# Cross-attention scores of a transformer block: one fp32 product against three products of rounded and remaining parts

## The chip, the cores and the metric

The kernel runs on one core of a Trainium2 chip. A core has five engines, each with its own instruction stream: TensorE (PE in the profile; matmuls and transposes, results into PSUM), VectorE (DVE), ScalarE (ACT), GpSimd (POOL), and SyncE (SP), which here only issues DMAs. They share an on-chip memory (SBUF) and wait for each other through semaphores. Within an engine, instructions run in the order in which the program lists them. PSUM has eight banks of 512 fp32 columns on 128 partitions.

The metric is the device time of one execution. Before the change: 1,482.18 us, the median of three runs (1,481.14 to 1,485.02).

## The reference

Eight batches of 512 tokens with 256 features, and a context of 64 rows a batch. In the cut, what matters is the first half:

```python
def _L0_xattn_ref(inputs_q, inputs_kv, Wq, bq, Wk, bk, Wv, bv, Wo, bo):   # H, HD = 16, 64
    q = jnp.einsum('bqm,mhd->bqhd', inputs_q, Wq) + bq
    k = jnp.einsum('bkm,mhd->bkhd', inputs_kv, Wk) + bk
    v = jnp.einsum('bkm,mhd->bkhd', inputs_kv, Wv) + bv
    q = q / jnp.sqrt(jnp.asarray(HD, q.dtype))
    attn = jax.nn.softmax(jnp.einsum('bqhd,bkhd->bhqk', q, k), axis=-1)
    out = jnp.einsum('bhqk,bkhd->bqhd', attn, v)
    return jnp.einsum('bqhd,hdm->bqm', out, Wo) + bo
...
x = x + _L0_xattn_ref(_layernorm(x), ctx_1024, ...)
x = x + _L0_ffn_ref(_layernorm(x), ...)   # dense path (causal attention, 16 heads of 16; SiLU FFN of 1024) + sparse path (8 experts, top 2)
```

## The kernel before

The batches are taken one after the other in eight *walks*, numbered 0 to 7, of about 143 us each; after the last comes a stretch with the experts and the final sum. Walk b handles the cross attention, the queries and keys, the routing and the maxima of batch b, and beside that the causal attention and the feed-forward network of batch b - 1. Walk 0 has no batch before it. The order of the steps is a list written by hand (`CROSS`, `SCORES`, `STEPS`), and every engine goes through the same list and does its own share of each step. So an instruction that waits holds up all that comes behind it on its engine.

The head of a walk is about the cross attention. Its scores are x times a folded matrix: for each pair of heads, the transposed query weights `wqT` times the block-diagonal keys `k_bd` of this batch. The steps are:

- `m` 0 to 3 (L871): the fold, each of four products into bank 0, 1, 2 or 3; the results go to `m_sb` in SBUF, 2 x 1024 columns. ScalarE copies `m` 0 and 2 (L1170), VectorE `m` 1 and 3 (L1432).
- `x_turn` 0 and 1 (L844): TensorE transposes the normalised x into banks 0 and 1, after the copies have freed them; ScalarE copies to `xnT` (L1146).
- `shift` 1 (L979): small transposes for the batch before (the row maxima of its second half of heads), in bank 5; VectorE copies them (L1555), SyncE sends them on.
- `bqk` (L880): bias products; `sc` (L996), `va` (L1009), `out_t` (L1020): scores, values and outputs of the causal attention of the batch before, put between the steps of the cross attention.
- `cs` t, half (L901): the cross scores of token tile t (four tiles of 128) and one half of the heads, two fp32 products of 128 rows of `xnT` by 512 columns of `m_sb` into one bank. The profile shows each fp32 product as two records. Both halves then go through VectorE (L1441 add, L1443 maximum, L1444 subtract), ScalarE (L1184 exponential), VectorE (L1451 sum, L1452 reciprocal) and GpSimd (L721 normalise); `ct` (L913) and `cv` (L920) are the transposes and the value products.

GpSimd also makes the causal cuts (L703) that `va` waits for, an addition of a bias to x (L716), and sums for the output. The feed-forward network's up projection (L1051) already multiplies in three products of a rounded part and a remaining part, in the type `float32r`; each product is one record of 512 columns. VectorE makes the remaining part of its input by a subtraction of the rounded part from the PSUM bank (L1570). At the end of a walk VectorE scales the feed-forward result (L1624).

Of the kernel before, what the change touches and what calls it, by code (L numbers as in the profile page):

```python
# [17 lines left out]
P = 128  # L18
# [33 lines left out]
    x_in=16, kv_in=64, stats=4, stats1=1, mv1=1, rstd1=1, xn1=1, xT1=2, xnT=2, bq=1,  # L52
    m_ps=4, m_act=2, m_dve=2, bqk_ps=2, bqk_sb=2, vw_ps=4, vw_sb=4,
# [4 lines left out]
    gmax=1, gexp=1, mask=1, rank_ps=1, slot=1, xk=1, scat=128, dve_step=42, pool_a=4, pool_n=1,  # L58
    a_ps=32, a_max=32, m_part=2, mT_ps=2, mT_sb=2, m_row0=48, m_row1=48,
    b_ps=G * UNITS, b_exp=G * UNITS, b_cut=G * UNITS, va_ps=G * CHUNKS, av_sb=4, avT_ps=4, o_rec=4, o_nrm=4,  # L60
    oT_ps=2, oT_sb=2, wo_ps=2, wo_sq=2, wo_ri=1, wo_n=2, hb=1, h=2, yb=1, hT_ps=2, hT_sb=2, hT_lo=2,
    fu_ps=16, fu_th=8, fu_u=8, fu_g=8, fd_ps=8, fd_sq=1, fd_ri=1, fd_n=1, y=1, y_out=16, pool_f=2,
# [144 lines left out]
def xattn_ffn(nc, A, out):  # L207
    per = PER
    counted = {}
    with ExitStack() as ctx:  # L210
# [10 lines left out]
        p0 = {n: sem("p0_" + n) for n in ("w_first", "bias_ps", "w_early", "w_mid", "w_late", "w_turned", "w_up", "kv0_ps", "norms", "split_hi", "split", "ident", "const", "iota", "tr_ps", "tr_sb", "kv_ps", "kv_sb", "bk")}  # L221

        moe = {n: sem("moe_" + n) for n in ("table_step", "table", "ids_off", "ids", "ew_in", "zero", "gate", "xT_ps", "xT", "up_ps", "th", "u", "g", "gT_ps", "gT", "dn_ps", "eo")}
# [43 lines left out]
        with nc.sbuf_tensor("hT", [P, 2, KD, S], F32R) as hT:  # L267
            pass
        room = sb("room", [P, 28672])
# [9 lines left out]
        m_sb = part(0, 2048).rearrange("p (k n) -> p k n", k=KD)  # L279
# [41 lines left out]
        w_heads = yb[:, :, :].rearrange("p t d -> p (t d)").rearrange("p (i k n) -> p i k n", i=2, k=KD)  # L321
        xnT = sb("xnT", [P, KD, S])
        xn2T = sb("xn2T", [P, KD, S])
# [68 lines left out]
        vt_d = internal("vt_d", (PAIRS, P, B * CK))  # L392
        parts_d = internal("parts_d", (3, 2, HD, H // KD, KD, S), BF16)
# [13 lines left out]
        def before(eng, b, name):  # L407

            if not (isinstance(b, int) and b == 0):
                eng.wait_ge(sems[name], b * per[name] + AHEAD.get(name, 0))  # L410

# [36 lines left out]
        def _(sp):  # L448
# [74 lines left out]
            def batch(b, c, end=False, only=None):  # L523
# [5 lines left out]
                if b is not None:  # L529
                    if c is None:  # L530
                        load_late_weights()
                    elif b != B - 1:
                        load_kv(b + 1)
# [13 lines left out]
                    send_shifts(b, 0)  # L547
                    if c is None:
# [59 lines left out]
        def _(pool):  # L608
# [44 lines left out]

            def batch(b, c, end=False, only=None):
# [1026 lines left out]
```

## Time and profile before

| | |
|---|---|
| median of the three runs | 1,482.18 us (1,481.14 to 1,485.02) |
| span of the profiled execution | 1,484.5 us, first to last instruction |
| runs' own times, in order | 1,485.02, 1,482.18, 1,481.14 us |
| TensorE busy, matmuls | 1,362.4 us, 92% |
| mean granted TensorE clock | 0.976 |

No separate time was taken around the profiled execution beside its span; the span is used for it. "Busy" is the time in which at least one instruction of the engine is shown running. Matmuls are pipelined, so two records in a row overlap by their tails: the start of one to the start of the next is what a product takes in a stream. A row of the view in order of time has the start, the length, the engine, the line, the operation, the names and shapes, and the count of instructions merged in it; in brackets stands the idle time ahead of it and what ended it.

### The profile page before, as it was taken

What the parts mean: (1) busy time and instruction counts of PE and PEld (TensorE: products, weight loads), DVE (VectorE), ACT (ScalarE), POOL (GpSimd) and SP (SyncE); (2) the same over time, 40 slices, a digit from 0 to 9 for tenths busy, and PEclk for the clock granted to TensorE, in tenths of its full rate; (3) what the DMA queues carried; (4) which work ended last, traced back from release to release, by engine and by line L of the source; (5) the groups of instructions that cost most, each with busy time, mean ns of one, the idle gap of its engine ahead of it and who ended that gap; (6) DMA issues with size and microseconds to landing.
All of it is one profiled execution on the core that took longest, in us unless ns stands there. A gap on an engine that the chain in (4) does not pass through costs nothing. (4 is left out here: it accounts for less than half of the span.)

```text
span 1484.5 us, 22385 instructions
## 1 busy us (share of the span) xinstructions
PE 1362.4 (92%) x7229; PEld 882.2 (59%) x7230; DVE 810.0 (55%) x1654; ACT 575.1 (39%) x1214; POOL 600.2 (40%) x1051
## 2 busy tenths in 40 slices
PE   6887899899999989998999899999999889999995
PEld 5543556666665666566656665666566346666674
DVE  2625554764585368536753675467537623333348
ACT  2231553055306521642265126503640443344446
POOL 4312353254325342634254225423542445555544
PEclk9998899999999999999999999999999899999997
DMA  6053204110501050106000500140022533322245
GB/s 213 1 153 132 86 1 121 52 30 1 142 30 30 1 156 16 30 8 160 20 15 30 141 17 15 51 121 17 1 83 74 162 107 128 129 87 85 85 186 193
DMA packets 78297, 115.39 MB, mean 78 GB/s; under 512 B 24840, under 2 KB 66208, under 8 KB 75648
## 3 DMA queue, kind: packets, MB, share of 16 engines
q1 hardware_dynamic: 67888, 79.69, 17.9%
q10 hardware_dynamic: 3840, 16.78, 4.2%
q0 software_dynamic: 6480, 17.77, 3.3%
q8 instruction: 52, 0.85, 0.2%
q14 instruction: 37, 0.30, 0.1%
HBM read 70.22 MB, written 43.59 MB: 77 GB/s over the span
## 5 line engine op out<-in xcount | busy, mean ns | idle before, releaser
L1540 DVE TENSOR_REDUCE nm<-ps 128x2 f32<-128x256 f32 (+3 forms) x256 | 202.5, 819 | 85.6 <-PE ps L970 79.5
L1229 ACT ACTIVATE room<-ps 128x512 f32<-128x512 f32 x320 | 179.8, 599 | 151.3 <-PE ps L996 151.1
L1051 PE MATMUL ps<-hT,w 128*128 128x512 f32 x768 | 206.5, 412 | 0.0
L703 POOL TENSOR_SCALAR_AFFINE_SELECT room<-room 128x256 f32<-128x256 f32 (+1 forms) x320 | 121.0, 390 | 136.4 <-ACT room L1229 131.7
L969 PE MATMUL ps<-room 96*128 96x128 bf16 (+3 forms) x512 | 127.9, 312 | 35.7 <-DMA room<-parts_d 17.8
L1051 PEld LDWEIGHTS ps<-hT,w 128*128 128x128 f32 x768 | 140.4, 190 | 32.1 <-DVE hT L1570 2.0
L1061 PE MATMUL ps<-w,room 128*128 128x256 f32 x512 | 137.8, 400 | 7.8 <-DVE room L1591 7.8
L1253 ACT ACTIVATE room<-ps 128x512 f32<-128x512 f32 x64 | 37.2, 593 | 277.2 <-PE ps L1051 277.2
L1087 PE MATMUL ps<-room 128*128 x284 | 135.4, 599 | 1.8 <-ACT room L1281 1.8
L920 PE MATMUL ps<-room 128*128 128x256 f32 x512 | 123.1, 384 | 2.8 <-ACT room L1190 1.8
L901 PE MATMUL ps<-room,xnT 128*128 128x512 f32 x256 | 122.0, 601 | 0.0
L996 PE MATMUL ps<-room 99*128 99x384 bf16 (+3 forms) x512 | 111.0, 306 | 8.7 <-ACT room L1229 6.4
L969 PEld LDWEIGHTS ps<-room 96*128 96x128 bf16 x512 | 50.9, 100 | 97.9 <-DVE nm L1540 41.1
L920 PEld LDWEIGHTS ps<-room 128*128 128x128 f32 x512 | 93.8, 190 | 22.7 <-issue 6.7
L1061 PEld LDWEIGHTS ps<-w,room 128*128 128x128 f32 x512 | 91.9, 195 | 24.1 <-DVE room L1591 11.5
L970 PE MATMUL ps<-mask_qk,ident_b 128*128 128x128 bf16 x512 | 104.6, 225 | 0.0
L1634 DVE COPY room<-ps 128x256 f32<-128x256 f32 x71 | 30.1, 424 | 125.9 <-PE ps L1095 117.7
L1441 DVE TENSOR_TENSOR room<-ps,room 128x1024 f32<-128x1024 f32 x32 | 39.1, 1222 | 106.0 <-PE ps L901 106.0
L996 PEld LDWEIGHTS ps<-room 99*128 99x128 bf16 x512 | 42.9, 98 | 88.0 <-issue 44.7
L1009 PE MATMUL ps<-room,v_aug 128*32 128x512 f32 (+3 forms) x1024 | 90.6, 449 | 3.0 <-POOL room L703 2.0
L652 POOL TENSOR_TENSOR spare_p<-neg_half 128x1 f32<-128x1 f32 x95 | 18.3, 192 | 179.7 <-DVE room L1533 114.6
L794 POOL DMA_INDIRECT pair_d<-room,ids_u x71 | 71.8, 1011 | 33.7 <-issue 30.5
(236 smaller groups left out, 2360.1 us busy)
## 6 DMA issues: line engine op xcount, KB each, us to landing
room<-parts_d SPq DMA_DIRECT2D x48, 256.0 KB, 8.7
room<-parts_d ACTq DMA_DIRECT2D x48, 256.0 KB, 6.2
room<-xs_d SPq DMA_DIRECT2D x71, 129.0 KB
parts_d<-room SPq DMA_DIRECT2D x64, 128.0 KB, 1.8
room<-pair_d SPq DMA_DIRECT2D x8, 1024.0 KB, 7.8
room<-in_L_ffn_ew SPq DMA_DIRECT2D x24, 256.0 KB, 5.5
xin<-in_x SPq DMA_DIRECT2D x8, 512.0 KB, 11.3
parts_d<-xnT SPq DMA_DIRECT2D x32, 128.0 KB, 1.8
```

The lines of the kernel that those rows point to most:

```text
L703: done(g.affine_select(out=w, in_=w, compare_op=ALU.is_ge, fill=0.0, base=0, pattern=[[0, 2]] * (blocks - 1) + [[1, P]], channel_multiplie ...
L901: last = mm(bank(half), xnT[:, k, t * P:(t + 1) * P], m_sb[:, k, half * 512:(half + 1) * 512], start=(k == 0), stop=(k == KD - 1))
L920: last = mm(bank(3, D), pT[:, t % 2, a * P:(a + 1) * P], vw[:, a, :], start=(a == 0), stop=(a == PAIRS - 1))
L969: mm(bank(o, n), q_rep[0:KREP, rep_at(h), t * P:n], k_rep[0:KREP, rep_at(h), 0:n], start=True, stop=False)
L970: last = mm(bank(o, P, t * P), ident_b[:, :], mask_qk[:, :], start=False, stop=True)
L996: last = mm(ps[:, o:o + S - kb * P], k_rep[0:KREP + MROWS, h, kb * P:(kb + 1) * P], q_rep[0:KREP + MROWS, h, kb * P:S], start=True, stop=T ...
L1009: last = mm(ps[32 * j:32 * j + 32, 4 * 512 + kb * P:5 * 512], v_aug[:, v_at(kb, 4 * grp + j):v_at(kb, 4 * grp + j) + 32], prob[:, at:at + ...
L1051: last = mm(bank(up_banks(b, m)[i]), w[:, x, k, m * P:(m + 1) * P], hT[:, y, k, :], start=((x, y, k) == terms[0]), stop=((x, y, k) == term ...
L1061: last = mm(bank((6, 7)[half], D, t % 2 * D), gT[:, m % 2, t * P:(t + 1) * P], w2[:, m, :], start=(m == 0 and t % 2 == 0), stop=(m == FB - ...
L1087: last = mm(bank(2 + i % 2), xsT[:, i % 2, k * P:(k + 1) * P], ew[:, bass.ds(at + k * 2 * D, 2 * D)], start=(k == 0), stop=(k == KD - 1))
L1229: done(fn(prob[:, u * 512:(u + 1) * 512], bank(score_bank(b) + n % 2), ACT.Exp), "b_exp")
L1540: done(v.tensor_reduce(nm[:, t, 2 * hp:2 * hp + 2], pair_ps, AX.X, ALU.max, negate=True), "a_max")
```

## The change

The cross scores are computed from a rounded part (`_hi`, type `float32r`) and a remaining part (`_lo`) of both x and the folded weights, by three products for each of the two depth blocks: hi x hi, lo x hi, hi x lo. For that, ScalarE now copies all four folds and both turns of x, rounding, and VectorE subtracts each copy from its bank. The turns of x use banks 4 and 5 and no longer wait for copies of the fold. The shift's transposes, in bank 5 too, wait for the remaining part of x. The remaining part of the folded weights is written over `wqT`, so `wqT` is kept in DRAM by a store in walk 0 and loaded again once a walk (walks 1 to 6); in walk 0 another place is used. Counters of VectorE's and GpSimd's inner steps, which had one semaphore for each purpose, now share one for each engine.

```diff
+        m_lo_first = over_room("m_lo_first", 22528, [P, PAIRS, D])
+        m_lo = over_room("m_lo", 7168, [P, PAIRS, D])
...
@@ SyncE
+                        sp.wait_ge(p0["tr_sb"], 6)
+                        sp.dma_start(wqT_d, wqT.rearrange("p a n -> p (a n)")).then_inc(p0["wq_kept"], 16)
...
                     send_shifts(b, 0)
+                    if c is not None and b != B - 1:
+                        need(sp, b, "sc_ps", T)
+                        sp.dma_start(wqT.rearrange("p a n -> p (a n)"), wqT_d).then_inc(p0["wq_in"], 16)
@@ TensorE
-                        turn(b, xh, (0, 1), lambda t2: [("xn1", 1), (("m_act", "m_dve")[t2], 1)], "xT1", step[1:])
+                        turn(b, xh, (4, 5), lambda t2: [("xn1", 1)], "xT1", step[1:])
...
+                            if b >= 2:
+                                pe.wait_ge(p0["wq_in"], 16 * (b - 1))
...
-                        need(pe, b, ("m_act", "m_dve")[i], 2)
+                        need(pe, b, "m_lo", 3 + i)
...
-                            need(pe, b, "m_act", 2)
-                            need(pe, b, "m_dve", 2)
-                            need(pe, b, "xnT", 2)
+                            need(pe, b, "m_lo", 4)
+                            need(pe, b, "xnT_lo", 2)
...
-                        for k in range(KD):
-                            last = mm(bank(half), xnT[:, k, t * P:(t + 1) * P], m_sb[:, k, half * 512:(half + 1) * 512], start=(k == 0), stop=(k == KD - 1))
+                        for x, y, k in [(x, y, k) for x, y in ((0, 0), (1, 0), (0, 1)) for k in range(KD)]:
+                            rows = m_low(b)[:, half * 4:half * 4 + 4, k * P:(k + 1) * P] if y else m_hi[:, k, half * 512:(half + 1) * 512].rearrange("p (a n) -> p a n", a=4)
+                            last = mm(bank(half).rearrange("p (a n) -> p a n", a=4), (xnT_hi, xnT_lo)[x][:, k, t * P:(t + 1) * P], rows,
+                                      start=((x, y, k) == (0, 0, 0)), stop=((x, y, k) == (0, 1, KD - 1)))
...
@@ TensorE, the shift's transposes
                             need(pe, b, "a_max", 19)
+                        elif b is not None:
+                            need(pe, b, "xnT_lo", 2)
@@ ScalarE
-                        spread(b, xnT, (0, 1), "xT1", "xnT", step[1:])
-                    elif kind == "m" and step[1] % 2 == 0:
+                        spread(b, xnT_hi, (4, 5), "xT1", "xnT", step[1:])
+                    elif kind == "m":
                         i = step[1]
                         need(act, b, "m_ps", i + 1)
-                        done(fn(m_sb[:, i // 2, 0:512], bank(i), ACT.Copy), "m_act")
+                        done(fn(m_hi[:, i // 2, i % 2 * 512:(i % 2 + 1) * 512], bank(i), ACT.Copy), "m_hi")
@@ VectorE
-                    elif kind == "m" and step[1] % 2:
+                    elif kind == "m":
                         i = step[1]
-                        need(dve, b, "m_ps", i + 1)
-                        done(v.tensor_copy(m_sb[:, i // 2, 512:1024], bank(i)), "m_dve")
+                        need(dve, b, "m_hi", i + 1)
+                        if b and i == 0:
+                            dve.wait_ge(p0["wq_kept"], 16)
+                        done(v.tensor_tensor(m_low(b)[:, i % 2 * 4:i % 2 * 4 + 4, i // 2 * P:(i // 2 + 1) * P], bank(i).rearrange("p (a n) -> p a n", a=4),
+                                             m_hi[:, i // 2, i % 2 * 512:(i % 2 + 1) * 512].bitcast(F32).rearrange("p (a n) -> p a n", a=4), ALU.subtract), "m_lo")
+                    elif kind == "x_turn":
+                        t2 = step[1]
+                        need(dve, b, "xnT", t2 + 1)
+                        cols = slice(t2 * 2 * P, (t2 + 1) * 2 * P)
+                        done(v.tensor_tensor(xnT_lo[:, :, cols], bank(4 + t2).rearrange("p (k n) -> p k n", k=KD),
+                                             xnT_hi[:, :, cols].bitcast(F32), ALU.subtract), "xnT_lo")
```

The order of TensorE at the head of a walk, before. Line numbers are those of the kernel before; a count stands behind the row, and in brackets what it waits for.

```order
L871 MATMUL ps<-room 128x128 [waits a_max]
L871 MATMUL ps<-room 128x128 x7
L844 MATMUL ps<-ident,room 128x128 [waits m_dve,xn1]
L844 MATMUL ps<-ident,room 128x128 x3
L979 MATMUL ps<-ident_b,nparts 128x128 [waits m_part]
L979 MATMUL ps<-ident_b,nparts 128x128 x3
L880 MATMUL ps<-room 128x128 [waits m_act,bq]
```

The same place after. L900 is the fold, L871 the turn of x, L1011 the shift's transposes, L909 the bias product (in the line numbers of the changed kernel).

```order
L900 MATMUL ps<-room 128x128 [waits a_max]
L900 MATMUL ps<-room 128x128 x7
L871 MATMUL ps<-ident,room 128x128 [waits xn1]
L871 MATMUL ps<-ident,room 128x128 x3
L1011 MATMUL ps<-ident_b,nparts 128x128 [waits xnT_lo,m_part]
L1011 MATMUL ps<-ident_b,nparts 128x128 x3
L909 MATMUL ps<-room 128x128 [waits m_lo,bq]
```

Nothing has moved on TensorE there; the waits are others. The turn has one less, the shift's transposes and the bias product wait for VectorE's subtractions.

VectorE at the same place, before: the scaling of the feed-forward result, two copies of the fold, the copy of the shift.

```order
L1551 TENSOR_TENSOR nparts<-nr,nparts 128x4x8 [waits dve_step]
L1624 SCALAR_TENSOR_TENSOR room<-ps,ri,fw_bc 128x256 [waits fd_ri]
L1624 SCALAR_TENSOR_TENSOR room<-ps,ri,fw_bc 128x256 x3
L1432 COPY room<-ps 128x512 [waits m_ps] x2
L1555 COPY mT<-ps 48x512 [waits mT_ps]
L1441 TENSOR_TENSOR room<-ps,room 128x1024 [waits bqk_sb,sc_ps]
```

And after, with the subtractions at L1456 (fold) and L1462 (x):

```order
L1653 SCALAR_TENSOR_TENSOR room<-ps,ri,fw_bc 128x256 [waits fd_ri]
L1653 SCALAR_TENSOR_TENSOR room<-ps,ri,fw_bc 128x256 x3
L1456 TENSOR_TENSOR m_lo<-ps,m_hi 128x4x128 [waits p0_wq_kept,m_hi]
L1456 TENSOR_TENSOR m_lo<-ps,m_hi 128x4x128 [waits m_hi]
L1462 TENSOR_TENSOR xnT_lo<-ps,xnT_hi 128x2x256 [waits xnT]
L1456 TENSOR_TENSOR m_lo<-ps,m_hi 128x4x128 [waits m_hi] x2
L1462 TENSOR_TENSOR xnT_lo<-ps,xnT_hi 128x2x256 [waits xnT]
L1585 COPY mT<-ps 48x512 [waits mT_ps]
L1472 TENSOR_TENSOR room<-ps,room 128x1024 [waits bqk_sb,sc_ps]
```

Six subtractions stand where two copies stood, between the scaling and the copy of the shift.

SyncE's queue late in a walk, after. L470 loads the next x, L484 sends the shift's rows, L570 is the added load, L593 stores the output of the batch before.

```order
L564 DMA room<-parts_d 16x8192 x5
L470 DMA xin<-in_x 128x4x256 [waits xn1,xb]
L484 DMA room<-mT 1x8x512 [waits mT_sb]
L484 DMA room<-mT 1x8x512 x2
L570 DMA room<-wqT_d 128x2048 [waits sc_ps]
L593 DMA y_d<-hb 128x1024 [waits y]
```

The load is between the sends of the first half of the shift and the store of the output.

## Rows read from the trace of the kernel before

**Rows 1.** Busy time and share of the span, by engine, with instruction counts.

```profile
PE 1362.4 (92%) x7229; PEld 882.2 (59%) x7230; DVE 810.0 (55%) x1654; ACT 575.1 (39%) x1214; POOL 600.2 (40%) x1051
```

**Rows 2.** TensorE's waits: who for whom, us in total, times, longest.

```profile
PE ps L1009 <- POOL room L703: 2.0, 7, 0.3
```

**Rows 3.** Instructions grouped by line: count, busy us, mean ns.

```profile
L901 PE MATMUL ps<-room,xnT 128*128 128x512 f32 x256 | 122.0, 601 | 0.0
```

**Rows 4.** TensorE in order of time, walk 3: cross scores and their successors.

```profile
456.34 1.94 PE L901 MATMUL ps<-room,xnT 128*128 128x512 f32 x4
458.11 0.60 PE L996 MATMUL ps<-room 99*128 99x384 bf16 x4
...
466.08 1.99 PE L901 MATMUL ps<-room,xnT 128*128 128x512 f32 x4
467.90 0.60 PE L996 MATMUL ps<-room 99*128 99x512 bf16 x2
```

**Rows 5.** TensorE in order of time, walk 3: up projection in three products.

```profile
531.03 5.87 PE L1051 MATMUL ps<-hT,w 128*128 128x512 f32 x24
...
568.51 1.64 PE L1051 MATMUL ps<-hT,w 128*128 128x512 f32 x6
569.99 0.23 PE L969 MATMUL ps<-room 96*128 96x128 bf16 x1
```

**Rows 6.** All engines in order of time, walk 3, behind the second tile's scores.

```profile
467.70 1.90 POOL L721 TENSOR_TENSOR room<-room,crec 128x1024 f32<-128x1024 f32 x1 [0.29 <-DVE crec L1452]
...
471.88 3.10 POOL L703 TENSOR_SCALAR_AFFINE_SELECT room<-room 128x128 f32<-128x128 f32 x6
...
472.49 1.06 PE L1009 MATMUL ps<-room,v_aug 128*32 128x512 f32 x8 [0.29 <-POOL room L703]
```

**Rows 7.** All engines in order of time, head of walk 3.

```profile
448.58 1.65 DVE L1624 SCALAR_TENSOR_TENSOR room<-ps,ri,fw_bc 128x256 f32<-128x256 f32 x4
...
450.16 0.68 DVE L1432 COPY room<-ps 128x512 f32<-128x512 f32 x1
...
451.16 0.69 DVE L1432 COPY room<-ps 128x512 f32<-128x512 f32 x1 [0.33 <-PE ps L871]
451.45 0.39 PE L979 MATMUL ps<-ident_b,nparts 128*128 128x128 bf16 x4
451.65 0.60 ACT L1146 ACTIVATE xnT<-ps 128x512 f32<-128x512 f32 x1 [0.78 <-PE ps L844]
```

**Rows 8.** VectorE in order of time, walk 3: subtraction of a rounded part.

```profile
529.69 1.29 DVE L1570 TENSOR_TENSOR hT<-ps,hT 128x512 fp32r<-128x512 f32 x2 [2.16 <-ACT hT L1146]
```

**Rows 9.** VectorE and TensorE in order of time, head of walk 1.

```profile
164.82 1.28 DVE L1432 COPY room<-ps 128x512 f32<-128x512 f32 x2
165.65 0.63 PE L844 MATMUL ps<-ident,room 128*128 128x128 f32 x4 [0.56 <-DVE room L1432]
166.12 0.39 PE L979 MATMUL ps<-ident_b,nparts 128*128 128x128 bf16 x4
```

**Rows 10.** SyncE's sends, the next fold, and loads of 1,024 KB (median us to landing).

```profile
576.05 2.06 SPq L466 DMA_DIRECT2D room<-mT  x3
...
589.61 2.02 PE L871 MATMUL ps<-room 128*128 128x128 f32 x16 [0.44 <-DVE nm L1540]
...
room<-in_L_ffn_w SPq DMA_DIRECT2D x2, 1024.0 KB, 6.9
...
room<-in_L_xattn_Wo SPq DMA_DIRECT2D x1, 1024.0 KB, 11.2
```

**Rows 11.** VectorE and TensorE in order of time, walk 0.

```profile
32.66 0.69 DVE L1432 COPY room<-ps 128x512 f32<-128x512 f32 x1 [3.19 <-PE ps L871]
...
34.69 3.60 PE L901 MATMUL ps<-room,xnT 128*128 128x512 f32 x8
...
56.70 0.65 PE L913 MATMUL ps<-ident,room 128*128 128x128 f32 x4 [1.29 <-DVE x L1457]
```

**Rows 12.** Two stretches: busy us by engine, granted clock, DMA share, GB/s.

```profile
156.00:158.00 2.00, 1.75 (x7) 0.90 (x8) 1.47 (x3) 0.00 (x0) 0.00 (x0) 0.50 0.58 238
545.50:548.70 3.20, 0.01 (x1) 0.00 (x0) 0.50 (x3) 0.60 (x1) 0.19 (x1) 1.00 0.70 168
```

More of the change, by code:

```diff
@@ L1371, in make_table @@
-                chain(v.tensor_reduce(expert, begun[:, :, :], AX.X, ALU.add))
-                chain(v.tensor_tensor(begun[:, :, :], begun[:, :, :], starts, ALU.mult))
-                chain(v.tensor_reduce(start, begun[:, :, :], AX.X, ALU.max))
-                chain(v.tensor_scalar(expert, expert, -1.0, None, ALU.add))
-                chain(v.tensor_tensor(row, tile_c, start, ALU.subtract))
-                chain(v.tensor_scalar(row, row, float(P), None, ALU.mult))
-                chain(v.scalar_tensor_tensor(row, expert, float(REG), row, ALU.mult, ALU.add))
@@ L1378, in make_table @@
-                chain(v.tensor_scalar(table[:, 0, :], expert, float(EW), None, ALU.mult))
-                chain(v.tensor_scalar(start, tile_no[:, :], total, None, ALU.is_lt))
-                chain(v.tensor_scalar(row, row, -float(E * REG), None, ALU.add))
-                chain(v.tensor_tensor(row, row, start, ALU.mult))
+                link(v.tensor_tensor(begun[:, :, :], tile_c.unsqueeze(2).to_broadcast(by_expert), starts, ALU.is_ge))
+                link(v.tensor_reduce(expert, begun[:, :, :], AX.X, ALU.add))
@@ new lines, in make_table @@
+                link(v.tensor_tensor(begun[:, :, :], begun[:, :, :], starts, ALU.mult))
+                link(v.tensor_reduce(start, begun[:, :, :], AX.X, ALU.max))
+                link(v.tensor_scalar(expert, expert, -1.0, None, ALU.add))
+                link(v.tensor_tensor(row, tile_c, start, ALU.subtract))
+                link(v.tensor_scalar(row, row, float(P), None, ALU.mult))
+                link(v.scalar_tensor_tensor(row, expert, float(REG), row, ALU.mult, ALU.add))
+                link(v.tensor_scalar(table[:, 0, :], expert, float(EW), None, ALU.mult))
@@ L1383, in make_table @@
+                link(v.tensor_scalar(start, tile_no[:, :], total, None, ALU.is_lt))
+                link(v.tensor_scalar(row, row, -float(E * REG), None, ALU.add))
+                link(v.tensor_tensor(row, row, start, ALU.mult))
                 v.tensor_scalar(table[:, 1, :], row, float(E * REG), None, ALU.add).then_inc(moe["table"], 1)
[L1384 to L1385 removed]
+                link(v.tensor_scalar(start, tile_no[:, :], total, None, ALU.is_ge))
@@ L1416, in batch @@
                             last = v.bn_stats(st1[:, t, :], xin[:, t, :])
-                        done(last, "stats1")
-                        need(dve, n, "stats1", 1)
+                        link(last)
                         carry_wait()
```

90 lines of the change are left out of this document (46 added, 44 removed).

## The prediction

> **What bounds the kernel now.** I read the shares of busy time first. TensorE is busy for 92% of the span, VectorE for 55%, ScalarE and GpSimd for about 40% [rows 1]. The chain of waits does not help here: it only follows the last few microseconds, in the mixing stage at the end. So I took the list of waits of TensorE and asked what it ever waits for. No item of it is large; a small one is to matter below, seven waits for GpSimd of 0.3 us at most [rows 2]. For the rest the walks are TensorE working through its own order. A microsecond of matmul that goes is worth a microsecond, unless the next thing in the order then waits; and a wait put in TensorE's order costs what it lasts.
>
> **The products.** A walk has eight score banks (four token tiles, two halves). Before, a bank is two fp32 products, shown as four records of 512 columns: 256 records in all, 122.0 us [rows 3]. The up projection already uses the three-product scheme, with one record a product. Busy time counts overlapping tails, so I price by start to next start. Two banks of the score line take 1.77 us (456.34 to 458.11) and 1.82 us (466.08 to 467.90) [rows 4]; the six others of that walk lie between 1.72 and 1.87, and 1.77 is the middle. A group of six products of the up projection takes 1.48 us (568.51 to 569.99) [rows 5]. The new bank is six such products with the same shapes and the same kind of operands, so I take 1.48, and a gain of 0.29 us a bank, 2.3 us a walk. Bounds: the run of 24 such products in 5.87 us with a last record of 0.39 gives a pitch of 0.238 us, hence 1.43 a bank and a gain of 0.34; the shortest old bank of 1.72 gives 0.24. The rows of the remainder of the folded weights are now read in four pieces of 128 columns with a step between them. No row shows such a read; I cost it at nothing and keep 0 to 0.05 us a bank in the range, since all else in the product is as in the up projection.
>
> The Trainium skill speaks of the rate too ("TensorE: Matmul & The Clock Gate", section "Wait — 56ns, not 53.3ns?"): back-to-back matmuls start every 215.7 ns at 512 columns. By that a bank would be 1.29 us, an estimate, and the gain 0.48 us. The rows give 0.238 to 0.25 for this very form, so they decide. The rival on cheap products below is what it would be otherwise.
>
> **Where a gain is not kept.** In walks 1 to 7 the attention of the batch before is interleaved. After the second tile's scores TensorE comes to a value product at 472.49 that already waits 0.29 us for GpSimd [rows 6]. GpSimd gets there by a chain of its own: the normalisation from 467.70 (1.90 us), the bias addition (2.38 us), then the causal cuts from 471.88 that the product needs. It starts from a reciprocal that hangs on the first tile and not on the second, whose matmuls run beside it. Two banks made shorter by 0.29 us make TensorE arrive 0.58 us sooner and wait 0.58 us longer. The seven waits of at most 0.3 us [rows 2] are this place in each of the seven walks. So six banks of eight pay: 6 x 0.29 = 1.74 us a walk. The other places have no such wait before; I looked at the cuts and exponentials behind each pair of banks and they end 0.1 us or more before they are needed.
>
> **What is added.** At the head of a walk, TensorE folds the weights (four groups), and turns x (two groups). Before, ScalarE and VectorE share the copies: ScalarE has four, VectorE two. After, ScalarE makes a rounded copy of all six and VectorE subtracts each of the six from its bank. TensorE then has, in its order, the small transposes of the shift. They now use a bank that the second turn of x occupies, so they wait for the sixth subtraction, and everything behind them waits with them: the bias products, the first scores of the previous batch, the cross scores.
>
> When does the sixth end? Take walk 3 [rows 7]. VectorE is late here: the scaling of the feed-forward output starts at 448.58 and holds it until the first copy at 450.16. Nothing of this is changed. The subtractions then follow back to back. Each has one input in PSUM, one in SBUF and 512 elements; the pair of the same form in the feed-forward stage takes 1.29 us for two [rows 8], so a pitch of 0.60 and 0.69 for the last. ScalarE is not later: the fourth fold is done when the second copy of VectorE is let go, at 451.16; ScalarE needs 0.6 us for it and 0.6 us more for the turn (the length of its copy at 451.65), 452.4, while VectorE gets to the sixth only at 453.16. So 450.16 + 5 x 0.60 + 0.69 = 453.85. In walk 1 a copy of VectorE that starts at 164.82 and ends about 165.5 lets a transpose of TensorE go at 165.65 [rows 9], so 0.15 us for the release: 454.0. Before, the transposes start at 451.45. The wait is 2.55 us. No work of TensorE fills it, as its order is fixed. Bounds: 2.3 (the queue of subtractions starts no earlier, but the release is free) to 3.1 us (a pitch of 0.69 instead of 0.60).
>
> Walk 1 is different and gives the same. VectorE there splits weights until 164.82, the two copies start then, and the transposes run at 166.12 [rows 9]. After: 164.82 + 3.69 + 0.15 = 168.66, 2.54 us later.
>
> Who else waits? What the shift writes is needed only by the third group of heads, well into the walk. The exponentials and cuts are let go by TensorE and move with it. GpSimd, which is behind at the head of a walk, has time to catch up, but its first cuts are not waited for in either case.
>
> **The reload.** The subtractions overwrite the transposed weights, so six times a 1,024 KB load is added on SyncE's queue, behind the three small sends that SyncE issues from 576.05 for 2.06 us. Its condition, the last scores, is long met. It is issued at about 578.1. TensorE folds at 589.61 [rows 10]: 11.5 us. The nearest 1,024 KB loads landed in 6.9 us, and in 11.2 us where a whole set of weights was loading at once; here the DMA is quiet. I take 7 us, which is hidden with 4 us to spare; at 11.2 us it would just be at the edge. What follows it in SyncE's queue is the store of the output, at the next walk's head. The first store of these weights, and the two new semaphores, wait for nothing that isn't long done. The other edits (shared counters in place of one for each step) change names, not the number of waits.
>
> **The first walk** has no attention beside it. The fourth fold is copied at 32.66 [rows 11]; now a rounded copy (0.60) and a subtraction (0.69) stand in a row there, to 33.95, and the second bias group starts after it at about 34.1 and takes about 1 us, so the scores start near 35.1 instead of 34.69: 0.4 us later. Two banks in a row are 3.60 us there and will be 0.39 + 11 x 0.238 = 3.01. Tile 0 gives 0.6 - 0.4, tile 1 gives 0.6, tile 3 gives 0.6, and tile 2 nothing, since TensorE waits 1.29 us behind it for VectorE [rows 11]. Together 1.4 us.
>
> **Sum.** Seven walks at 2.55 - 1.74 = 0.81 are 5.7 us; less 1.4 us, so 4.3 us slower. The profiled execution has a span of 1,484.5 us, 2.3 us above the median of 1,482.18 and just under the highest run. From 1,484.5 the sum leads to 1,488.8; the same 4.3 us on the median give 1,486.5, and that is the forecast. It is 0.29%, so it lies on the edge: I count over 0.3% (4.4 us) as what a measurement of this kernel can tell from no change.
>
> **Rivals.**
> *Cheap products (faster).* If a product of the new form starts every 0.215 us, half of the pitch of an old record ((3.60 - 0.59) / 7 = 0.43 [rows 11]), a bank is 1.29 and gains 0.48. Seven walks at 2.55 - 2.88 = -0.33 are -2.3, the first walk -2.2, together -4.5: 1,477.7. For it: nothing but that the columns allow it. Against: the run of 24 [rows 5]. It decides below 0.22 us.
> *Every bank pays.* If the wait for GpSimd moves with TensorE, 0.58 x 7 = 4.1 us come back: 1,482.4, no change. Against: GpSimd is busy without a gap from 467.70 to 472.49.
> *A longer wait.* At 3.1 us in place of 2.55 the seven walks lose 3.9 us more: 1,490.4. For it: six dependences across three engines, each a possible 0.1 us.
> *The reload is late.* From 11.5 us on, each microsecond costs six: 14 us would make 1,501. Against: the quiet DMA.
> *The clock falls.* A granted clock of 0.50, the lower level of 1.2 GHz, stands at 156 to 158 us [rows 12], in the first walk's end, where TensorE had waited again and again. If the new idle did this in each walk and it lasted 3 us, it would cost 1.5 us, 7 x 1.5 = 10.5: 1,497. Against: TensorE is idle for 3.2 us in walk 3 (545.5 to 548.7), after steady work, and the clock is 1.00 in that stretch [rows 12]. The Trainium skill (the same page, section "HAM oscillation — how this bites in real kernels") says that idle gaps throttle the engine again; by that rule a longer gap than this might do it, and the trace shows that one of 3.2 us did not.
>
> **How the numbers follow.** Forecast 0.50 (0.30 of it within 0.3%, 0.20 beyond); every bank pays 0.13 (no change); cheap products 0.15 (faster); longer wait 0.13, late reload 0.05, clock 0.04 (slower). So faster 0.15, same 0.43, slower 0.42. The forecast's own range, with 0.24 to 0.34 a bank and 2.3 to 3.1 us of wait, is 1,482 to 1,493; to hold eight of ten it has to reach into the faster rival and over the longer wait: 1,479 to 1,493.
>
> **What would show it.** Per walk: the score products busy for about 13 us instead of 15.4; TensorE idle for 2.5 us before the shift's transposes, released by VectorE's sixth subtraction; the wait for GpSimd before the value product grown from 0.3 to 0.9 us; no wait for the reloaded weights before the fold. I am wrong if the transposes start less than 2 us after the second turn, if a bank takes under 1.4 or over 1.6 us, or if the fold waits for a DMA.

## The result, and the profile after

| | before | after |
|---|---|---|
| median, us | 1,482.31 (20 runs) | 1,488.95 (20 runs) |
| lowest to highest, us | 1,474.4 to 1,489.83 | 1,480.97 to 1,503.78 |
| span of the profiled execution, us | 1,484.5 | 1,486.7 (its own time 1,488.45) |
| ratio after to before, with its 95% interval | | 1.0042 [1.0025, 1.0059] |

The changed kernel is slower by 0.42%, about 6.2 us, with 3.7 to 8.7 us as the interval. The forecast was 4.3 us and 1,486.5, its range 1,479 to 1,493: the time lies in it. Slower had a chance of 0.42, no change (within 0.3%) one of 0.43, faster 0.15. The prediction saw the two mechanisms and came near their sizes; it missed a third, which the experiments below bring out. The run of 1,503.78 us, over 1.5% above the fastest, is not in the ratio.

Busy time by engine, the row that answers to [rows 1]:

```profile
PE 1345.9 (91%) x7357; PEld 904.4 (61%) x7358; DVE 828.7 (56%) x1686; ACT 583.2 (39%) x1230; POOL 601.7 (40%) x1051
```

TensorE is busy for 16.5 us less than before [rows 1], and yet the span is 2.2 us longer. So TensorE's idle time grew by 18.7 us. The waits of TensorE (who for whom, us in total, times, longest) say where:

```profile
PE ps L1011 <- DVE xnT_lo L1462: 18.5, 7, 3.6
...
PE ps L999 <- DMA room<-parts_d: 15.1, 7, 3.3
...
PE ps L1041 <- POOL room L730: 6.2, 7, 0.9
```

The first is new: 18.5 us before the shift's transposes. The third was 2.0 us [rows 2]. The second stands in both kernels (14 to 18 us in the traces of either) and varies from one execution to the next; where I compare walks below, I take it out.

The score products, grouped by line and names, answer to [rows 3]:

```profile
L930 PE MATMUL ps<-m_hi,xnT_hi 128*128 128x512 f32 x128 | 46.7, 446 | 0.0
L930 PE MATMUL ps<-m_hi,xnT_lo 128*128 128x512 f32 x128 | 40.2, 395 | 0.0
L930 PE MATMUL ps<-m_lo,xnT_hi 128*128 128x512 f32 x112 | 35.2, 395 | 0.0
L930 PE MATMUL ps<-m_lo_first,xnT_hi 128*128 128x512 f32 x16 | 5.0, 395 | 0.0
```

There are 384 records where there were 256. The busy times of the four groups add up to 127.1 us, more than the 122.0 before, but records of two groups overlap and are counted in both. All records of the line taken together are busy for less (us, TensorE, weight load, granted clock, DMA share, GB/s):

```profile
0.00:1487.00 1487.00, 105.75 (x384) 68.86 (x384) 0.97 0.27 83
```

That is 13.2 us a walk where it was 15.2, and 16.2 us less in all, nearly all that TensorE's busy time lost. TensorE in order of time at the head of walk 3 (start, length, count, and in brackets the idle time before it):

```profile
447.35 2.02 PE L900 MATMUL ps<-room 128*128 128x128 f32 x16 [0.44 <-DVE nm L1570]
...
454.52 0.38 PE L1011 MATMUL ps<-ident_b,nparts 128*128 128x128 bf16 x4 [2.48 <-DVE xnT_lo L1462]
...
457.12 0.76 PE L930 MATMUL ps<-m_hi,xnT_hi 128*128 128x512 f32 x2
...
459.08 0.71 PE L930 MATMUL ps<-m_hi,xnT_hi 128*128 128x512 f32 x2
459.63 0.63 PE L930 MATMUL ps<-m_hi,xnT_lo 128*128 128x512 f32 x2
460.09 0.63 PE L930 MATMUL ps<-m_lo,xnT_hi 128*128 128x512 f32 x2
460.56 0.61 PE L1028 MATMUL ps<-room 99*128 99x384 bf16 x4
```

This bank runs from 459.08 to 460.56, 1.48 us, against 1.77 in [rows 4]. From start to next start the eight banks of the walk take 1.48 to 1.60 us, where they took 1.72 to 1.87. The transposes wait 2.48 us. What VectorE does meanwhile, against [rows 7]:

```profile
449.14 1.65 DVE L1653 SCALAR_TENSOR_TENSOR room<-ps,ri,fw_bc 128x256 f32<-128x256 f32 x4
450.71 1.28 DVE L1456 TENSOR_TENSOR m_lo<-ps,m_hi 128x512 fp32r<-128x512 f32 x2
451.90 0.68 DVE L1462 TENSOR_TENSOR xnT_lo<-ps,xnT_hi 128x512 fp32r<-128x512 f32 x1
452.50 1.27 DVE L1456 TENSOR_TENSOR m_lo<-ps,m_hi 128x512 fp32r<-128x512 f32 x2
453.69 0.68 DVE L1462 TENSOR_TENSOR xnT_lo<-ps,xnT_hi 128x512 fp32r<-128x512 f32 x1
```

Six subtractions without a gap, 3.66 us from the first start to the last end; 0.15 us after it the transposes start. And behind the second tile, all engines in order of time, against [rows 6]:

```profile
470.17 1.91 POOL L748 TENSOR_TENSOR room<-room,crec 128x1024 f32<-128x1024 f32 x1 [0.28 <-DVE crec L1483]
...
474.35 3.10 POOL L730 TENSOR_SCALAR_AFFINE_SELECT room<-room 128x128 f32<-128x128 f32 x6
...
474.95 1.07 PE L1041 MATMUL ps<-room,v_aug 128*32 128x512 f32 x8 [0.89 <-POOL room L730]
```

TensorE waits 0.89 us there where it waited 0.29. From the normalisation to the value product it is 4.78 us, as before (467.70 to 472.49): GpSimd's chain is as long as it was, and TensorE comes to its end sooner. The reload, among the DMA issues (KB each, median us to landing):

```profile
room<-wqT_d SPq DMA_DIRECT2D x6, 1024.0 KB, 4.9
```

In walk 3 it is issued at 580.11 for the fold at 591.55; the median of the six lands 4.9 us after its issue. No wait of TensorE for it is listed.

### The profile page after: what moved, and what is told of

Same layout as the page of the kernel before. It is cut to its first block and busy times, and to the rows that moved or that the text cites. A ratio compares the mean times of both kernels' runs of the same rounds, so it can differ in the third digit from the quotient of the medians.

```text
span 1486.7 us, 22694 instructions
## 1 busy us (share of the span) xinstructions
PE 1345.9 (91%) x7357; PEld 904.4 (61%) x7358; DVE 828.7 (56%) x1686; ACT 583.2 (39%) x1230; POOL 601.7 (40%) x1051
## 5 line engine op out<-in xcount | busy, mean ns | idle before, releaser
L1083 PEld LDWEIGHTS ps<-hT,w 128*128 128x128 f32 x768 | 141.8, 192 | 32.4 <-DVE hT L1599 2.0
L950 PEld LDWEIGHTS ps<-room 128*128 128x128 f32 x512 | 93.8, 190 | 22.0 <-issue 5.8
L1663 DVE COPY room<-ps 128x256 f32<-128x256 f32 x71 | 30.1, 424 | 125.8 <-PE ps L1127 125.8
L1028 PEld LDWEIGHTS ps<-room 99*128 99x128 bf16 x512 | 39.7, 99 | 75.3 <-issue 38.2
L1119 PEld LDWEIGHTS ps<-room 128*128 128x128 f32 x284 | 50.3, 189 | 45.8 <-issue 41.2
```

The costliest lines, as they stand in the source:

```text
L950: last = mm(bank(3, D), pT[:, t % 2, a * P:(a + 1) * P], vw[:, a, :], start=(a == 0), stop=(a == PAIRS - 1))
L1028: last = mm(ps[:, o:o + S - kb * P], k_rep[0:KREP + MROWS, h, kb * P:(kb + 1) * P], q_rep[0:KREP + MROWS, h, kb * P:S], start=True, stop=T ...
L1083: last = mm(bank(up_banks(b, m)[i]), w[:, x, k, m * P:(m + 1) * P], hT[:, y, k, :], start=((x, y, k) == terms[0]), stop=((x, y, k) == term ...
L1119: last = mm(bank(2 + i % 2), xsT[:, i % 2, k * P:(k + 1) * P], ew[:, bass.ds(at + k * 2 * D, 2 * D)], start=(k == 0), stop=(k == KD - 1))
```

## The experiments

For walks I give the length from one fold's start to the next, of the shortest walk in which the granted clock stays at 1.00, less TensorE's wait for the DMA in it; I call that the clean walk. It is 139.6 us before (142.81 less 3.2, walk 3) and 140.3 after (141.98 less 1.7, walk 4): the new walk is 0.7 us longer. Not every walk at full clock is as short: a wait of TensorE for VectorE in the feed-forward stage is 0.5 us in these two, and 1.6 in walk 4 before and 1.5 in walk 2 after. It varies in both kernels.

### Is it the wait for the sixth subtraction?

**e1_swap.** The two turned halves of x change banks, so that the transposes' bank hangs on the first half and the third subtraction.

```diff
-  turn(b, xh, (4, 5), ...)            # TensorE
+  turn(b, xh, (5, 4), ...)
-  need(pe, b, "xnT_lo", 2)            # before the shift's transposes
+  need(pe, b, "xnT_lo", 1)
-  spread(b, xnT_hi, (4, 5), ...)      # ScalarE
+  spread(b, xnT_hi, (5, 4), ...)
-  v.tensor_tensor(xnT_lo[...], bank(4 + t2)...)
+  v.tensor_tensor(xnT_lo[...], bank(5 - t2)...)
```

> The changed kernel with the two turns of x in banks 5 and 4 instead of 4 and 5, so that the shift's transposes (bank 5) wait for the third of the six subtractions and not for the sixth. If VectorE's queue of subtractions sets the head of the walk: the wait before the shift falls from 2.5 to about 0.8 us, new waits of about 0.4 us each come before the bias products or the first score bank, and the scores start 1.2 to 1.4 us earlier in walks 1 to 7: 8 to 10 us less than the changed kernel, so about 2 to 4 us below the kernel before. If the reload or the shared counters cost the time: the same time as the changed kernel.

Measured: 1,476.44 us (12 runs), ratio to the kernel before 0.996 [0.9938, 0.9981]; so 12.5 us less than the changed kernel by the medians. TensorE, head of walk 3:

```profile
443.64 2.02 PE L900 MATMUL ps<-room 128*128 128x128 f32 x16 [0.44 <-DVE nm L1570]
...
449.02 0.38 PE L1011 MATMUL ps<-ident_b,nparts 128*128 128x128 bf16 x4 [0.70 <-DVE xnT_lo L1462]
449.62 1.13 PE L909 MATMUL ps<-room 128*128 128x128 f32 x8 [0.21 <-DVE m_lo L1456]
...
452.02 0.76 PE L930 MATMUL ps<-m_hi,xnT_hi 128*128 128x512 f32 x2
```

The wait is 0.70 and not 2.48 us, and from fold to scores it takes 8.38 us (9.77 after, 7.38 before). The clean walk is 138.8 us, 1.4 less. Six such walks are 8.5 us. Walk 1 gives more, 3.3 us (145.70 for 149.00): its wait goes from 3.57 to 1.53 us, and with it goes a fall of the clock (below).

### What are the products alone worth?

**e2_products.** The kernel before, with six rounded products a bank in place of the fp32 ones. The products of the remaining parts, and the making of those parts, are left out (the rounded product is run three times).

```diff
-  for k in range(KD):
-      last = mm(bank(half), xnT[...], m_sb[...], ...)
+  for r, k in [(r, k) for r in range(3) for k in range(KD)]:
+      last = mm(bank(half), xnT_hi[...], m_hi[...], ...)
```

> The kernel before, but each score bank made by six products of the rounded part of x and of the rounded folded weights (the remaining parts are left out, the same rounded operands taken three times). No subtraction, no reload, banks and waits as before. If the products gain 0.29 us a bank and two banks of eight are lost to the wait for GpSimd: 7 x 1.74 + about 2 to 3 in the first walk, 14 to 15 us less than before, with the wait for GpSimd at 0.9 us. If all eight banks pay: 18 to 19 us less. If the products gain nothing: no change.

Measured: 1,463.43 us (6 runs), ratio 0.9884 [0.985, 0.9918], 17 us less by the ratio and 18 by the medians. The time alone is nearer to my "all eight banks pay" (18 to 19) than to "two are lost" (14 to 15). The trace decides. The wait for GpSimd in the list of TensorE's waits:

```profile
PE ps L1013 <- POOL room L706: 6.3, 7, 0.9
```

The wait for GpSimd grows to 0.9 us with the products alone, so it is they that uncover it. The clean walk is 137.7 us, 1.9 less than before; I had 1.74. Laid beside the kernel before, what follows a bank in walk 3 comes 0.30 to 0.33 us sooner for each of the eight banks, 2.5 us in all, and 0.60 goes at the wait for GpSimd: 1.9. So a bank gives a little more than my 0.29, and two banks of eight are lost, as forecast. Seven walks are 13 us, and walk 0 is 4.8 us shorter (130.31 for 135.12). Of that, 1.4 us lie ahead of its scores and 2.4 in a wait for ScalarE at its end (2.38 for 4.74 us), which is 3.05 us in e7_bias_only with the old products; so some of it belongs to that one execution of before and not to the products. The price of the subtractions, 140.3 less 137.7, is 2.6 us a walk.

### Does the reload cost anything?

**e3_reload.** The kernel before, with the store of the transposed weights, the six reloads, the fold's wait for them, and the shared counters.

```diff
+  sp.dma_start(wqT_d, wqT.rearrange("p a n -> p (a n)"))...
...
+  if c is not None and b != B - 1:
+      need(sp, b, "sc_ps", T)
+      sp.dma_start(wqT.rearrange("p a n -> p (a n)"), wqT_d)...
...
+  if b >= 2:
+      pe.wait_ge(p0["wq_in"], 16 * (b - 1))
```

> The kernel before with the store of the transposed weights, the reload once a walk and the shared counters, and nothing else of the change. If the reload is hidden: no wait for it before the fold, and the time of the kernel before within 0.3%. If the reload or the counters are what makes the changed kernel slower: about 6 us more than before.

Measured: 1,481.69 us (12 runs), ratio 0.9995 [0.9975, 1.0015]. The reload landed in 4.9 us here too, and no wait of TensorE for it is listed. It costs nothing that this can tell, which is from 3.7 us less to 2.2 more.

### Is it the length of the wait?

**e6_two_more.** The changed kernel, with each of the two subtractions of x made twice: two more instructions in VectorE's queue, one of them ahead of the fourth, both ahead of the transposes.

```diff
+  link(v.tensor_tensor(xnT_lo[:, :, cols], bank(4 + t2)..., xnT_hi[:, :, cols]..., ALU.subtract))
   done(v.tensor_tensor(xnT_lo[:, :, cols], bank(4 + t2)..., xnT_hi[:, :, cols]..., ALU.subtract), "xnT_lo")
```

> The changed kernel with each of the two subtractions of x made twice by VectorE, so two more in the queue of six. If that queue sets the head of the walk: the wait before the shift grows from 2.5 by 1.2 to 1.5 us in walks 2 to 7, 8 to 10 us more than the changed kernel, about 1,498 us. If a wait of that length also lets TensorE's clock fall to the lower level, as it did behind the wait of 3.6 us in walk 1 of the changed kernel (0.50 from 166 to 170 us), each walk in which that happens takes about 2 us more: up to 1,510 us, and the granted clock behind the shift shows 0.5. If ScalarE or a release sets the head: the time of the changed kernel.

Measured: 1,509.21 us (5 runs), ratio 1.0168 [1.0137, 1.0198]. In TensorE's waits:

```profile
PE ps L1011 <- DVE xnT_lo L1464: 29.7, 7, 6.0
```

That is 11.2 us more than after in seven waits (six of 3.94 or 3.95 us, 1.46 more each), but the time is 20 us more by the medians (19 by the ratios). The shortest walk less its wait for the DMA is 143.3 us (145.0 less 1.7), 3.0 longer, twice what the wait adds. So something is paid beside the wait. The next section has it.

### The clock behind the wait

**a1_again, a2_again, a3_again.** The changed kernel once more in three executions, unedited, to see whether the clock falls behind the transposes.

> The changed kernel once more, unchanged, for another profile. If the waits of 2.5 us before the shift let the clock fall in some executions and not in others, a granted clock of 0.5 stands behind the shift's transposes in one or more of walks 2 to 7 in some of the three. If only longer waits (3.6 us in walk 1, over 3 us for the DMA) do it, none of walks 2 to 7 shows it there, and the falls stand behind the DMA waits as in the kernel before.

> A second further profile of the unchanged changed kernel, with the same expectations as a1_again: a fall of the clock behind a 2.5 us wait of walks 2 to 7, or falls behind longer waits alone.

> A third further profile of the unchanged changed kernel, with the same expectations as a1_again: a fall of the clock behind a 2.5 us wait of walks 2 to 7, or falls behind longer waits alone.

Measured: 1,493.01, 1,494.96 and 1,491.85 us, with spans of 1,491.2, 1,493.2 and 1,490.1; the kernel before ran in 1,483.17 beside them (one run each, and not on the chip of the other experiments). First the four microseconds behind the transposes' start in the profiled execution of after, walks 1 and 3 (length; busy us of TensorE, weight load, VectorE, ScalarE, GpSimd; granted clock; DMA share; GB/s):

```profile
165.78:169.78 4.00, 4.00 (x24) 3.51 (x24) 0.42 (x1) 1.36 (x3) 0.29 (x1) 0.62 0.03 6
...
454.52:458.52 4.00, 4.00 (x29) 3.40 (x29) 0.42 (x1) 2.61 (x5) 1.72 (x3) 1.00 0.23 90
```

The five other walks show 1.00 as well. The same stretch of all seven walks in a2_again:

```profile
168.04:172.04 4.00, 4.00 (x20) 3.85 (x21) 0.42 (x1) 1.08 (x2) 0.29 (x1) 0.50 0.03 6
315.19:319.19 4.00, 4.00 (x29) 3.40 (x29) 0.42 (x1) 2.61 (x5) 1.72 (x3) 1.00 0.23 90
457.74:461.74 4.00, 4.00 (x22) 3.73 (x23) 0.42 (x1) 1.09 (x3) 1.41 (x2) 0.60 0.23 90
601.60:605.60 4.00, 4.00 (x29) 3.41 (x29) 0.42 (x1) 2.60 (x5) 1.73 (x3) 1.00 0.25 95
743.46:747.46 4.00, 4.00 (x22) 3.56 (x23) 0.42 (x1) 1.22 (x3) 1.43 (x2) 0.60 0.23 90
891.44:895.44 4.00, 4.00 (x24) 3.72 (x24) 0.42 (x1) 1.19 (x3) 1.43 (x2) 0.62 0.23 90
1038.22:1042.22 4.00, 4.00 (x24) 3.71 (x24) 0.42 (x1) 1.19 (x3) 1.43 (x2) 0.63 0.23 90
```

TensorE is busy without a gap in both, but in four of walks 2 to 7 it does 22 to 24 matmuls where it does 29 at full clock. TensorE in order of time there, walk 3 of a2_again:

```profile
457.74 0.59 PE L1011 MATMUL ps<-ident_b,nparts 128*128 128x128 bf16 x4 [2.49 <-DVE xnT_lo L1462]
458.12 2.02 PE L909 MATMUL ps<-room 128*128 128x128 f32 x8
...
461.78 0.81 PE L930 MATMUL ps<-m_hi,xnT_hi 128*128 128x512 f32 x2
```

From the transposes to the scores it is 4.04 us, against 2.60 in the profiled execution (454.52 to 457.12, the start of its first record of scores), after a wait of the same length to 0.01 us. In the eleven falls of walks 2 to 7 in the three traces, fold to scores takes 1.0 to 1.6 us more; in six of them it is 1.40 to 1.55, and a fall that comes late runs on behind the first scores. I counted the falls at this place in all four executions:

| execution | walk 1 | falls in walks 2 to 7 | span, us |
|---|---|---|---|
| after | 0.62 | 0 | 1,486.7 |
| a3_again | 0.57 | 4 (0.61, 0.57, 0.66, 0.63 in walks 3, 5, 6, 7) | 1,490.1 |
| a1_again | 0.62 | 3 (0.59, 0.57, 0.64 in walks 3, 5, 6) | 1,491.2 |
| a2_again | 0.50 | 4 (0.60, 0.60, 0.62, 0.63 in walks 3, 5, 6, 7) | 1,493.2 |
| e1_swap (waits of 1.5 and 0.7 us) | 1.00 | 0 | 1,470.8 |
| e6_two_more (waits of 6.0 and 3.9 us) | 0.50 | 6 (0.50 to 0.59) | 1,503.5 |

In e6_two_more all walks fall: 1.46 + 1.5 = 3.0 us a walk, the 3.0 found above. In e1_swap none does, not even in walk 1: there 3.3 us go, which with the 8.5 us of the six others makes 11.8, against 12.5 between the medians and 12.2 by the ratios.

The falls at this place can't simply be added to the span, because the clock falls behind the waits for the DMA too, with the old products as with the new. In walk 3 of after it does:

```profile
549.10:552.40 3.30, 3.21 (x11) 2.34 (x12) 1.02 (x2) 0.00 (x0) 1.08 (x1) 0.50 0.10 33
```

The three other executions have their fall of walk 3 behind the transposes and none later in that walk, and all four walks are equally long, 141.7 to 141.8 us less the wait for the DMA, 1.5 above the clean walk. So in this walk one fall took the place of the other. All falls have to be counted. Here is the time at the lower level (0.50) from the transposes of walk 1 to the fold of walk 7:

| execution | at the lower level, us | falls behind the transposes in walks 2 to 6 | length of walks 2 to 6, us |
|---|---|---|---|
| before | 13.7 | | 716.4 |
| e3_reload | 17.1 | | 716.9 |
| e7_bias_only (below) | 13.7 | | 713.2 |
| after | 20.5 | 0 | 719.5 |
| a3_again | 17.1 | 3 | 718.2 |
| a2_again | 30.1 | 3 | 723.0 |
| a1_again | 27.3 | 3 | 723.6 |

On the mean of these few executions the new kernel spends 9 us more at the lower level, 24 against 15. At half the clock that is at most 4.5 us of time, part of it in walk 1. But a3_again is shorter than after in these walks, with three falls at the transposes against none; its span is longer because its first fold starts at 27.59 and not at 23.12 us.

### Can the rest be had back?

**e4_swap_bias.** e1_swap, and GpSimd's addition of the bias to x behind the third tile's cut rather than ahead of the second value product, which waits for GpSimd.

```diff
-  ... ("vw", 3), ("sum", 0), ("x_bias",),
+  ... ("vw", 3), ("sum", 0),
-  ("cs", 2, 0), ("sum", 1), ...
+  ("cs", 2, 0), ("x_bias",), ("sum", 1), ...
```

> e1_swap, and GpSimd's bias addition (2.38 us) moved in the step list from before the second tile's scores to behind the first half of the third tile's. If GpSimd's chain of normalisation, bias addition and cuts is what the value product waits for: that wait of 0.9 us goes in walks 1 to 7, 5 to 6 us less than e1_swap, about 8 us below before. If another link of the chain holds the cuts: the wait stays and the time is that of e1_swap.

Measured: 1,472.34 us (8 runs), ratio 0.9932 [0.9906, 0.9958], 4 us less than e1_swap. The wait for GpSimd at the value product is gone from TensorE's list, and the one for ScalarE before the previous batch's scores has grown from 6.5 us in 16 waits to 7.6 in 22. The clean walk is 138.1 us, 0.7 less. In its walk 1 the wait before the transposes is 2.53 us, and the clock falls behind it (0.64); in the six others, with 0.70, it doesn't. **e7_bias_only**, the same move in the kernel before, asks whether that is worth anything there.

> The kernel before, with GpSimd's bias addition moved as in e4_swap_bias and nothing else. If the wait for GpSimd before the value product is all that it costs there: 0.3 us in each of seven walks, 2 us less than before, inside 0.3%; the same move was worth 0.9 us a walk or less once the products were shorter. If the addition holds more than that (a normalisation or a cut further on): more than 4 us less, or some us more.

Measured: 1,481.61 us (12 runs, of which one took 4,659.23 and is not in the ratio), ratio 0.9988 [0.9966, 1.0011]: nothing that can be told. In the kernel before this wait was only 0.3 us, so the same move had 2 us to gain there, less than the times can tell (its clean walk is 139.2 us, 0.4 less than before); with the faster products it gave 4 us.

**e5_bias_banks.** e4_swap_bias, with the bias products in the banks of the first two folds, where they wait for the first two subtractions only, and the shift's transposes between the two bias groups.

```diff
-  ("x_turn", 1), ("shift", 1), ("bqk", 0), ("bqk", 1),
+  ("x_turn", 1), ("bqk", 0), ("shift", 1), ("bqk", 1),
-  need(pe, b, "m_lo", 3 + i)
-  last = mm(bank(2 + i, P, a * P), ...)
+  need(pe, b, "m_lo", 1 + i)
+  last = mm(bank(i, P, a * P), ...)
+  if t == 0:                             # the scores take these banks next
+      need(pe, b, "bqk_sb", half + 1)
-  fn(bqk[...], bank(2 + i), ACT.Copy)
+  fn(bqk[...], bank(i), ACT.Copy)
```

> e4_swap_bias, with the bias products of the walk's head in banks 0 and 1, which the first two subtractions free, in place of 2 and 3, and the first of them listed ahead of the shift's transposes; the first scores wait for the copies of the bias products instead. If TensorE's idle time at the head is VectorE's queue of six subtractions: the bias product fills the wait, about 0.9 us of it goes in each of seven walks, 6 us less than e4_swap_bias, near 1,466 us. If something else there is last (ScalarE's copies of the bias products, now ahead of the scores), the wait moves to the first score bank and the time is that of e4_swap_bias.

Measured: 1,459.77 us (5 runs), ratio 0.9839 [0.981, 0.9868]: 24 us less than before, 29 less than the change as it was. TensorE, head of walk 3:

```profile
437.03 2.02 PE L900 MATMUL ps<-room 128*128 128x128 f32 x16 [0.43 <-DVE nm L1572]
...
442.66 0.39 PE L1013 MATMUL ps<-ident_b,nparts 128*128 128x128 bf16 x4
442.89 1.11 PE L909 MATMUL ps<-room 128*128 128x128 f32 x8
444.20 0.71 PE L932 MATMUL ps<-m_hi,xnT_hi 128*128 128x512 f32 x2
```

No wait for a subtraction is left, and fold to scores takes 7.17 us, less than before the change. The clean walk is 136.8 us, 1.3 less than e4_swap_bias, 9 us in seven; I had expected 6 in all. The medians are 12.6 us apart, the two profiled spans 12.4. Walk 1 is shorter by 2.7 us (144.19 for 146.85): the fall behind its transposes is gone. With six clean walks, 7.8 us, that makes 10.5 of the 12.6. The stretch from the last fold to the end is 4.8 us shorter in the two traces, 3.5 more than its clean walk. There the clock is at the lower level for longer in e4_swap_bias than in e5_bias_banks, at the same place of the program:

```profile
1148.40:1162.00 13.60, 12.96 (x65) 3.67 (x64) 11.50 (x34) 7.90 (x15) 7.89 (x15) 0.50 0.31 103
...
1139.40:1142.70 3.30, 3.24 (x15) 0.64 (x14) 2.80 (x14) 1.56 (x3) 1.44 (x4) 0.50 0.60 188
```

This differs between executions of all kernels (in e1_swap and e7_bias_only there is no fall there, in before and after one of 10.2 us), so I don't count it for the edit. The edit moves both the banks and the order of the steps; which of the two gives the gain was not tested.

## Why the prediction was right, and where not

**The products.** 1.48 us a bank was forecast; the banks of walk 3 take 1.48 to 1.60, and what follows them comes 0.30 to 0.33 us sooner for each (0.29 forecast, 0.24 to 0.34 the bounds). The pieces of 128 columns cost nothing: in e2_products, which reads without them, the last bank takes 1.48 too. e2_products gives 1.9 us a walk for 1.74. The sign named for it came as well: 13.2 us of score products a walk for "about 13". The rival of cheap products falls with it: no bank took 1.29 us.

**Two banks lose their gain to GpSimd.** The wait was to grow from 0.29 to 0.87 us and is 0.89; e2_products shows the same 0.9 without the subtractions, and e4_swap_bias that the 0.6 us come back when GpSimd is asked sooner. The rival in which every bank pays falls.

**The wait before the transposes.** 2.55 us were forecast, 2.48 measured in six walks. (The two reasons given for the bounds lead to 2.4 and 3.0, not to 2.3 and 3.1; nothing hangs on it.) e1_swap and e6_two_more show that it follows the queue of subtractions, in both directions. The longer wait of the third rival didn't come.

**Walk 1** was to be the same and is not: the wait is 3.57 us in the profiled execution, 3.49 to 4.47 in the others. I had left TensorE where it was and moved only VectorE. TensorE in order of time there:

```profile
161.62 0.60 PE L871 MATMUL ps<-ident,room 128*128 128x128 f32 x4
165.78 0.38 PE L1011 MATMUL ps<-ident_b,nparts 128*128 128x128 bf16 x4 [3.57 <-DVE xnT_lo L1462]
```

The turns no longer wait for the copies of the fold ([rows 9]: 0.56 us for VectorE) and run on, so TensorE is ready at about 162.2 and stands longer. A wait taken away ahead of a new wait lengthens it. The transposes themselves are hardly later than forecast: from the fold, 10.45 us for 7.69, which is 2.8 where I had 2.54. What the longer wait brought is the fall of the clock behind it.

**The reload** was to take 7 us and be hidden; it takes 4.9, and e3_reload puts its cost at nothing. **The first walk** was to gain 1.4 us. It is 2.9 us shorter in the profiled execution (132.21 for 135.12), and walk 1 gives 1.8 back (149.0 for 147.2). Over the traces walk 0 takes 132.2 to 134.0 us in the four of the new kernel and 134.8 to 137.2 in the three with the old products, 2.6 less on the mean. The forecast start of the scores (35.1) isn't confirmed: they start at 33.46, 35.26, 35.89 and 39.15, by where the clock is low and when the first fold starts.

**The sum per walk** was +0.81 and is +0.7 in a clean walk. The whole, as means of the four traces of the new kernel less the means of the three with the old products (before, e3_reload, e7_bias_only):

| stretch | forecast, us | traces, us |
|---|---|---|
| walk 0 | -1.4 | -2.6 |
| walk 1 | +0.8 | +2.1 |
| walks 2 to 6 | +4.1 | +5.6 |
| from the last fold on | +0.8 | +0.8 |

Counted from the first fold on, they add up to 5.9 us, near the 6.2 of the ratio and 1.6 above the forecast of 4.3. It is in part luck that the forecast came so near: walk 0 gained 1.2 us more than I had, and walk 1 lost 1.3 more. In walks 2 to 6 the clean walks account for 3.4 of the 5.6 us; the rest is the clock and the waits for the DMA, which these few traces don't part.

**The weak step is the rival of the clock**, to which I gave 0.04. I priced a fall rightly, at 1.5 us, and dismissed it, since in [rows 12] TensorE was idle for 3.2 us after steady work and the clock was 1.00. It was still 1.00 behind that wait. But it was one of seven waits for the DMA in the same trace, and behind three of the others the clock was at the lower level: behind 3.00 us in walk 1, 3.77 in walk 5, and 2.34 in walk 6. The stretch behind the wait of [rows 12], and walk 6 during its wait and behind it:

```profile
549.00:553.00 4.00, 4.00 (x27) 2.93 (x25) 2.97 (x5) 0.00 (x0) 2.05 (x2) 1.00 0.10 34
...
977.20:979.50 2.30, 0.01 (x1) 0.00 (x0) 0.50 (x3) 0.60 (x1) 0.19 (x1) 1.00 0.89 220
980.70:984.00 3.30, 3.30 (x11) 2.18 (x11) 1.58 (x3) 0.00 (x0) 1.50 (x2) 0.50 0.12 40
```

So the trace that the prediction had already showed that an idle of 2.3 us can be followed by a fall, and that the clock during the idle doesn't tell. The new waits do the same: one of 2.49 us in a2_again is followed by 0.60 in walk 3 and by 1.00 in walk 4, and in after by 1.00 in both. How many falls a timed run had wasn't seen. Their mean granted clocks go the same way as their times in the extremes (1,480.97 us at 0.977, 1,495.36 at 0.967), which shows the clock's part in the scatter and not the part of the new waits in it.

The Trainium skill ("TensorE: Matmul & The Clock Gate", section "HAM oscillation — how this bites in real kernels") describes a kernel whose clock falls after every wait for the DMA, with a penalty at each. Its figures, 26.7 us over 32 such waits, come to 0.83 us a wait, which is an estimate. The traces here agree on the kind, waits for the DMA with falls behind them, and not on the size: a fall costs about 1.5 us (walk 3). Nor does it come every time: it comes behind some waits of 2.5 us and not behind others.

## What to carry to other kernels

Price a new idle of TensorE by its length and by the work behind it at half clock. Before you dismiss a fall, look behind every wait of about that length in the trace that you have, and then in several executions. And count all falls, not those at the new place: one of them can stand where another would have come. When the banks of PSUM are handed to a new reader, ask which of them the next step on TensorE takes: here the same six subtractions cost 2.5, 1.1 or 0 us a walk between fold and scores (9.77, 8.38 and 7.17 us against 7.26 without them), by the bank and the order in which the transposes and bias products stood. And when products get shorter, look at who was only just in time before: 0.29 us of wait at one place foretold that a quarter of the gain would go.

## What the hardware showed that I had not expected

- Behind waits of 0.7 and 1.5 us before the transposes the clock stayed at 1.00 (13 of 13, in e1_swap and e4_swap_bias), and without a wait too (7 of 7 before, 7 of 7 in e5_bias_banks). Behind waits of 3.5 us and more it fell each time (11 of 11, in walk 1 of the four executions and in e6_two_more). Behind waits of 2.5 us it fell in 11 of 24, in the same program and with the same wait to 0.01 us: 0 of 6 in after and 11 of 18 in the three others. Whether the chip has a part in that was not tested.
- A walk with one such fall is 1.5 us longer: walk 3 is 141.7 us for the 140.3 of the clean walk, with the fall at its head (three executions) or behind the wait for the DMA (after).
- A 1,024 KB load lands in 4.9 us where the DMA share was 0.03 in the four microseconds up to 580, against the 6.9 and 11.2 us of [rows 10].
